# A new order of the deep layers' instruction queues, with blocks of value matmuls in pairs

## The reference

```
for i in range(6):
    x = attn_layer(shift_tokens(x), Wqkv[i], q_scale[i], k_scale[i], Wo[i]) + x
    x = ffn_layer(shift_tokens(x), ln_g[i], ln_b[i], W1[i], b1[i], W2[i], b2[i]) + x
# attn_layer: q, k, v = split(x @ Wqkv), 16 heads of 64
#             q, k = rotary(l2norm(q) * qs), rotary(l2norm(k) * ksc)
#             sim = 8 * q @ k.T   in windows of 32 with the window before
#             softmax(mask(sim)) @ v, then @ Wo
# ffn_layer:  xn = layernorm(x); a, gate = split(xn @ W1 + b1)
#             (a * gelu(gate)) @ W2 + b2
```

## Time and profile before

| | |
|---|---|
| median of 3 runs | 3265.14 us (3257.32 to 3265.72) |
| the profiled execution | 3262.19 us |
| its span, first to last instruction | 3260.4 us |
| PE busy | 3129.7 us, 96% |
| PEld busy | 2384.6 us, 73% |
| DVE busy | 2687.9 us, 82% |
| ACT busy | 2717.7 us, 83% |
| POOL busy | 2560.2 us, 79% |
| PE's share of the chain that ended last | 93% |
| granted TensorE clock, mean | 0.995 of full speed |

### The profile page before, as it was taken

How to read it: one execution, slowest core, us unless ns; L and a number is a source line. 1 busy time by engine, 2 the same in 40 slices (tenths; PEclk the granted TensorE clock), 3 DMA queues, 4 the chain that set the end, 5 groups by cost and what they waited for, 6 DMA issues and landing times.

```text
span 3260.4 us, 154019 instructions
## 1 busy us (share of the span) xinstructions
PE 3129.7 (96%) x65394; PEld 2384.6 (73%) x66148; DVE 2687.9 (82%) x4034; ACT 2717.7 (83%) x4817; POOL 2560.2 (79%) x2557
## 2 busy tenths in 40 slices
PE   8998799999999999999999999999999999999998
PEld 6886577777777777777777777777777777677776
DVE  6887888888888888888888888888888888788884
ACT  5665688888888888888888888888888888888886
POOL 3433988888888888888888888887888888788882
PEclk9999999999999999999999999999999999999999
DMA  1000332232233223223322322322332332332231
GB/s 47 29 2 28 83 79 73 75 78 68 71 75 86 69 71 80 70 64 88 82 61 74 79 67 77 85 70 63 78 78 72 78 75 67 86 75 62 65 76 52
DMA packets 140219, 224.69 MB, mean 69 GB/s; under 512 B 29456, under 2 KB 41360, under 8 KB 139152
## 3 DMA queue, kind: packets, MB, share of 16 engines
q1 hardware_dynamic: 139536, 214.78, 25.8%
HBM read 21.72 MB, written 4.19 MB: 8 GB/s over the span
## 4 chain that ended last, share of the span: by engine, by line
PE 93%; issue 3%; DVE 1%; POOL 1%; ACT 1%; DMA 0%; SPq 0%; POOLq 0%; DVEq 0%; ACTq 0%
PE bank L1021 12%; PE bank L954 11%; PE bank L906 11%; PE bank L1037 10%; PE bank L980 9%; PE bank L1367 8%; PE bank L907 7%; PE bank L999 5%; PE bank L1380 4%; PE bank L905 3%; PE bank L364 2%; PE bank L344 2%; PE bank L329 2%; PE bank L1352 1%; PE bank L1342 1%
## 5 line engine op out<-in xcount | busy, mean ns | idle before, releaser
L1284 POOL TENSOR_TENSOR rotbuf<-mbuf 128x512 f32<-128x512 f32 x768 | 975.1, 1275 | 340.4 <-PE bank L954 326.2
L1173 DVE TENSOR_TENSOR mbuf<-bank,table 128x512 f32<-128x512 f32 x768 | 522.5, 680 | 341.2 <-ACT sq L1063 290.0
L1298 POOL TENSOR_TENSOR rotbuf<-rotbuf,rs 128x512 f32<-128x512 f32 x768 | 788.9, 1043 | 14.9
L1063 ACT ACTIVATE sq<-bank 128x512 f32<-128x512 f32 x768 | 458.8, 597 | 154.7 <-PE bank L907 140.4
L1174 DVE TENSOR_TENSOR mbuf<-bank,table 128x512 f32<-128x512 f32 x768 | 522.8, 681 | 0.0
L906 PE MATMUL bank<-weights,inputs 128*128 128x512 bf16 x1152 | 438.4, 381 | 70.3 <-issue 45.3
L1021 PEld LDWEIGHTS bank<-probs_t,vbuf 64*64 64x64 f32 x24576 | 394.5, 134 | 115.7 <-issue 115.1
L954 PE MATMUL bank<-ident,rotbuf 128*128 128x128 f32 x3072 | 449.3, 279 | 17.6 <-POOL rotbuf L1298 7.8
L1155 DVE TENSOR_REDUCE ss<-sq 128x16 f32<-128x1024 f32 x384 | 459.4, 1196 | 0.0
L907 PE MATMUL bank<-weights,inputs 128*128 128x512 bf16 x1152 | 438.2, 380 | 0.0
L1021 PE MATMUL bank<-probs_t,vbuf 64*64 64x32 f32 x24576 | 437.3, 220 | 0.1
(11 more groups left out here) (119 smaller groups left out, 5736.5 us busy)
## 6 DMA issues: line engine op xcount, KB each, us to landing
vbuf<-v_stage SPq DMA_DIRECT2D x1152, 128.0 KB, 2.4
vbuf<-v_stage SPq DMA_DIRECT2D x576, 64.0 KB, 2.1
stage<-in_wqkv SPq DMA_DIRECT2D x36, 256.0 KB, 3.0
weights<-in_wo SPq DMA_DIRECT2D x6, 512.0 KB, 3.9
out_t<-weights SPq DMA_DIRECT2D x1, 2048.0 KB, 6.3
weights<-out_t SPq DMA_DIRECT2D x1, 2048.0 KB, 11.5
out_t<-weights SPq DMA_DIRECT2D x16, 128.0 KB, 2.0
wffn<-in_w SPq DMA_DIRECT2D x6, 341.0 KB, 3.1
```

Of the source, the lines that this page charges most:

```text
L1173: e.tensor_tensor(b.m1[:, u % 2, :].rearrange("p (h s d) -> p h s d", h=8, s=2), pj, cos, ALU.mult)
L1284: e.tensor_tensor(b.rot[:, u, :], b.m1[:, u % 2, :], b.m2[:, u % 2, :], ALU.add).then_inc(s.rotated, 1)
L1298: e.tensor_tensor(v, v, r, ALU.mult).then_inc(s.scaled, 1)
```

## The change

Every queue of the deep part except SP's gets a new order, and `WORK_RING` and POOL's reach follow it. No step is added or taken out, and no step changes inside. In the old order each small block on TensorE, of values or of scores, stands between large matmuls. In the new one the value blocks may stand in pairs, 128 matmul records together, and score blocks still stand alone: V2 and V3 follow each other, and V0 and V1. Of the diff, the lines that pair the value blocks, and POOL's reach:

```diff
 def pe_deep_slot(e, s, b, at):
...
-    pe_ff_mean(e, s, b, at, -1)
+    pe_ff_variance(e, s, b, at, -1)
     pe_values_of(e, s, b, at, 0, 2)
-    pe_project_in(e, s, b, at, 3, 1)
-    pe_ff_variance(e, s, b, at, -1)
     pe_values_of(e, s, b, at, 0, 3)
-    pe_ff_down(e, s, b, at, -2)
     pe_transpose(e, s, b, at, 2, 0)
...
+    pe_project_in(e, s, b, at, 3, 7)
     pe_values_of(e, s, b, at, 1, 0)
+    pe_values_of(e, s, b, at, 1, 1)
+    pe_transpose(e, s, b, at, 2, 7)
...
-POOL_REACH = (-1, 3)
+POOL_REACH = (-2, 3)
```

More of the change, by code:

```diff
@@ L1597, in pe_deep_slot @@
 def pe_deep_slot(e, s, b, at):
[L1599 to L1602, removed]
+    pe_values_in(e, s, b, at, 2, 1)
     pe_project_in(e, s, b, at, 3, 0)
     pe_transpose_probs_of(e, s, b, at, 0, 2)
-    pe_transpose(e, s, b, at, 1, 7)
+    pe_project_in(e, s, b, at, 3, 1)
+    pe_ff_mean(e, s, b, at, -1)
     pe_scores_of(e, s, b, at, 1, 1)
+    pe_ff_down(e, s, b, at, -2)
     pe_transpose_probs_of(e, s, b, at, 0, 3)
-    pe_values_in(e, s, b, at, 2, 1)
-    pe_ff_mean(e, s, b, at, -1)
+    pe_ff_variance(e, s, b, at, -1)
     pe_values_of(e, s, b, at, 0, 2)
-    pe_project_in(e, s, b, at, 3, 1)
-    pe_ff_variance(e, s, b, at, -1)
     pe_values_of(e, s, b, at, 0, 3)
-    pe_ff_down(e, s, b, at, -2)
     pe_transpose(e, s, b, at, 2, 0)
-    pe_transpose(e, s, b, at, 2, 1)
     pe_project_in(e, s, b, at, 3, 2)
@@ L1619, in pe_deep_slot @@
     pe_values_in(e, s, b, at, 2, 2)
+    pe_transpose(e, s, b, at, 2, 1)
+    pe_scores_of(e, s, b, at, 1, 3)
     pe_values_in(e, s, b, at, 2, 3)
-    pe_scores_of(e, s, b, at, 1, 3)
     pe_transpose(e, s, b, at, 2, 2)
     pe_transpose(e, s, b, at, 2, 3)
+    pe_values_in(e, s, b, at, 3, 0)
     pe_project_in(e, s, b, at, 3, 3)
@@ L1626, in pe_deep_slot @@
     pe_project_out(e, s, b, at, 0)
-    pe_values_in(e, s, b, at, 3, 0)
     pe_transpose(e, s, b, at, 2, 4)
+    pe_transpose_probs_of(e, s, b, at, 1, 0)
+    pe_transpose(e, s, b, at, 2, 5)
     pe_project_in(e, s, b, at, 3, 5)
-    pe_transpose(e, s, b, at, 2, 5)
-    pe_transpose_probs_of(e, s, b, at, 1, 0)
     pe_ff_up(e, s, b, at, -1, 0)
     pe_scores_of(e, s, b, at, 2, 0)
+    pe_transpose(e, s, b, at, 2, 6)
+    pe_transpose_probs_of(e, s, b, at, 1, 1)
     pe_ff_up(e, s, b, at, -1, 1)
@@ L1635, in pe_deep_slot @@
     pe_project_in(e, s, b, at, 3, 6)
-    pe_transpose_probs_of(e, s, b, at, 1, 1)
+    pe_ff_up(e, s, b, at, -1, 2)
+    pe_project_in(e, s, b, at, 3, 7)
     pe_values_of(e, s, b, at, 1, 0)
+    pe_values_of(e, s, b, at, 1, 1)
+    pe_transpose(e, s, b, at, 2, 7)
 def act_deep_slot(e, s, b, at):
[L1642 to L1651, removed]
+    act_copy_v(e, s, b, at, 2, 0)
     act_square(e, s, b, at, 2, 3)
     act_square(e, s, b, at, 2, 4)
+    act_input_of(e, s, b, at, 3)
     act_mask(e, s, b, at, 1, 0)
-    act_input_of(e, s, b, at, 3)
     act_ff_affine(e, s, b, at, -2)
     act_exp_of(e, s, b, at, 0, 1)
-    act_copy_v(e, s, b, at, 2, 0)
     act_copy_t(e, s, b, at, 1, 4)
+    act_copy_pt_of(e, s, b, at, 0, 0)
@@ L1660, in act_deep_slot @@
+    act_copy_t(e, s, b, at, 1, 5)
     act_square(e, s, b, at, 2, 5)
-    act_copy_t(e, s, b, at, 1, 5)
-    act_copy_pt_of(e, s, b, at, 0, 0)
-    act_ff_shift(e, s, b, at, -1)
[L1664 to L1668, removed]
+    act_ff_gelu(e, s, b, at, -2, 0)
+    act_copy_t(e, s, b, at, 1, 6)
+    act_ff_gelu(e, s, b, at, -2, 1)
+    act_copy_pt_of(e, s, b, at, 0, 1)
@@ L1669, in act_deep_slot @@
+    act_square(e, s, b, at, 2, 6)
+    act_ff_shift(e, s, b, at, -1)
     act_square(e, s, b, at, 2, 7)
     act_ff_gelu(e, s, b, at, -2, 2)
+    act_copy_t(e, s, b, at, 1, 7)
+    act_copy_v(e, s, b, at, 2, 1)
     act_square(e, s, b, at, 3, 0)
+    act_seed(e, s, b, at, 2)
+    act_square(e, s, b, at, 3, 1)
     act_copy_pt_of(e, s, b, at, 0, 2)
+    act_ff_square(e, s, b, at, -1)
     act_copy_out(e, s, b, at, 0, 0)
-    act_copy_t(e, s, b, at, 1, 7)
-    act_seed(e, s, b, at, 2)
     act_copy_pt_of(e, s, b, at, 0, 3)
-    act_copy_v(e, s, b, at, 2, 1)
@@ L1678, in act_deep_slot @@
-    act_ff_square(e, s, b, at, -1)
-    act_square(e, s, b, at, 3, 1)
     act_ff_seed(e, s, b, at, -1)
+    act_mask(e, s, b, at, 1, 1)
+    act_copy_t(e, s, b, at, 2, 0)
+    act_square(e, s, b, at, 3, 2)
+    act_exp_of(e, s, b, at, 1, 0)
+    act_copy_v(e, s, b, at, 2, 2)
+    act_copy_t(e, s, b, at, 2, 1)
+    act_copy_out(e, s, b, at, 0, 1)
+    act_copy_v(e, s, b, at, 2, 3)
+    act_copy_t(e, s, b, at, 2, 2)
+    act_copy_t(e, s, b, at, 2, 3)
 def dve_deep_slot(e, s, b, at):
-    dve_clamp(e, s, b, at, 2)
@@ L1686, in dve_deep_slot @@
     dve_rope(e, s, b, at, 3, 0)
+    dve_ff_centre(e, s, b, at, -1)
     dve_max_of(e, s, b, at, 1, 0)
-    dve_ff_centre(e, s, b, at, -1)
+    dve_rope(e, s, b, at, 3, 1)
     dve_shift(e, s, b, at, 1, 0)
-    dve_rope(e, s, b, at, 3, 1)
     dve_ff_refine(e, s, b, at, -1)
@@ L1694, in dve_deep_slot @@
     dve_sum_squares(e, s, b, at, 3, 0)
+    dve_rope(e, s, b, at, 3, 2)
     dve_sum_of(e, s, b, at, 1, 0)
-    dve_rope(e, s, b, at, 3, 2)
     dve_max_of(e, s, b, at, 1, 1)
@@ L1700, in dve_deep_slot @@
     dve_rope(e, s, b, at, 3, 4)
+    dve_sum_squares(e, s, b, at, 3, 1)
     dve_residual_of(e, s, b, at, 0)
-    dve_sum_squares(e, s, b, at, 3, 1)
+    dve_sum_of(e, s, b, at, 1, 1)
     dve_rope(e, s, b, at, 3, 5)
-    dve_sum_of(e, s, b, at, 1, 1)
-    dve_sum_squares(e, s, b, at, 3, 2)
     dve_ff_gate(e, s, b, at, -1, 0)
     dve_ff_gate(e, s, b, at, -1, 1)
+    dve_sum_squares(e, s, b, at, 3, 2)
     dve_rope(e, s, b, at, 3, 6)
+    dve_ff_gate(e, s, b, at, -1, 2)
     dve_rope(e, s, b, at, 3, 7)
-    dve_ff_gate(e, s, b, at, -1, 2)
     dve_sum_squares(e, s, b, at, 3, 3)
+    dve_clamp(e, s, b, at, 3)
 def pool_deep_slot(e, s, b, at):
+    pool_scale(e, s, b, at, 1, 3)
     pool_scale(e, s, b, at, 1, 4)
+    pool_rotate(e, s, b, at, 2, 1)
+    pool_normalise_of(e, s, b, at, 0, 0)
+    pool_rotate(e, s, b, at, 2, 2)
+    pool_ff_norm(e, s, b, at, -2)
     pool_scale(e, s, b, at, 1, 5)
+    pool_scale(e, s, b, at, 1, 6)
     pool_rotate(e, s, b, at, 2, 3)
+    pool_scale(e, s, b, at, 1, 7)
+    pool_rotate(e, s, b, at, 2, 4)
+    pool_normalise_of(e, s, b, at, 0, 1)
+    pool_rotate(e, s, b, at, 2, 5)
     pool_input_of(e, s, b, at, 3)
[L1720 to L1724, removed]
     pool_rotate(e, s, b, at, 2, 6)
@@ L1732, in pool_deep_slot @@
     pool_scale(e, s, b, at, 2, 2)
[L1733 to L1737, removed]
 def sp_deep_slot(e, s, b, at):
```

## The result

The changed kernel takes 3529.95 us (median of 4 runs, 3523.34 to 3539.99) where the kernel before took 3261.23 in the same runs: a ratio of 1.0828, 95% interval 1.0814 to 1.0842. I had forecast 3269, in a range of 3222 to 3304. The prediction was wrong, and by a term that is not in its sum.

The account below looks back on a forecast made before the run. TensorE, busy 96% of the span, was taken to bound the kernel. Paired value blocks -43, late instruction pages +54, today's stops -13, pages inside pairs +2, a freed bank +4 gave +4 us: forecast 3269, range 3222 to 3304.

Parts of the forecast that it names:

- Other moves: All queues: only places move, counts stay; one tight chain, the mean's bank freed by line 1470, charged +4 us.
- the same sum that I made for S3: TensorE's distance from the fourth value block's end to the fourth score block: 3.21 us in the new order, 5.33 before.
- Rival 2: Instruction pages behind the fourth value block held longer, most slots losing 2.1 us, not 1.7: 3296 us, chance 0.25.
- Rival 3: Bank of the mean freed 0.2 us late by line 1470 in every slot, +18 instead of +4: 3283 us, chance 0.08.
- The pairs: TensorE's paired value blocks save entries, ways out and longer following blocks: 0.48 us a slot, -43 us, from -25 to -50.
- Late pages: TensorE stops at the fourth score block, its instruction packet held behind SP's copies: +54 us in some 32 slots.
- +54 and -13 and +2: New stops for late instruction pages +54 us; today's stops not paid again -13; pages running out inside paired blocks +2.
- Rival 1: Instruction pages not late, as fewer fetches meet SP's group of copies or arrive ahead of it: 3226 us, chance 0.24.

Follow-up runs that it names:

- the changed order with its ring opened: Changed kernel, with ScalarE's copy of line 1095 waiting only for the five transfers that read its own half of the staging buffer, not all ten: 3230.69 us, 0.9918.

## Why the prediction was wrong, step by step

- **Other moves: the step that failed.** It said that "the counts of instructions and copies on ACT, DVE, POOL and SP stay; only places move, and SP's order stays as it is", and followed one chain, that of line 1470. That chain was harmless (0.2 us by its name at a projection). The move that cost 294 us in this order (89 in the old one) was costed at nothing, without naming its cover: v0 ahead of the output projection. What I left out could be worked out, in sign though not in size, from rows I had. SP's group begins at V3's end and issues a transfer every 0.63 us, so the tenth begins some 5.8 us after V3; that the first five had landed helped nobody, because line 1094 waits for all ten. From its issue a transfer takes 2.1 to 2.4 us to land, by the page of the kernel before (the last number; the tenth is one of 64 KB):

```profile
vbuf<-v_stage SPq DMA_DIRECT2D x1152, 128.0 KB, 2.4
vbuf<-v_stage SPq DMA_DIRECT2D x576, 64.0 KB, 2.1
```

With 0.6 for the copy the bank is free 8.5 to 8.8 us after V3. Before, it was a later transpose group that took v0's bank. Now it was the output projection, due 7.5 us after V3 by the same sum that I made for S3: 3.21, S3 and v3 1.4, two transposes 0.9, three projections 1.95. The difference, 1.0 to 1.3, is a wait in every slot, about 100 us; 2.37 a slot was measured. On average over the 90 slots the tenth transfer was issued only 7.0 us after V3, since one or two of the ten issues took over 0.9 us; the copy began 2.5 us later, and the projection was due at 7.8. What makes an issue take longer is not shown. The lower clock came on top.
- **None of the rivals was it.** Rival 2, worse late pages, was a mechanism of some tens of microseconds. Rival 3 was a bank that is freed late, but another bank and 18 us.
- **The pairs: right, and mis-sized.** -57 us instead of -43, outside the bounds of -25 to -50. The second block of a pair costs less than I took: 0.95 and 1.05 us for the two, 2.00 instead of 2.04; and the down projection behind S1 costs 1.40 us where I took 1.47. V2 and V3 stand as 128 records in 2.0 us, as said.
- **Late pages: the right kind, the wrong cause and size.** I had +54 and -13 and +2, +43 net; measured, +19. The packet that I placed at 3.2 us after V3's end starts in the new order mostly at 1.0 to 2.1, so S3 is stopped for 12 us and not for 54, and S2, which I left out, for 13. V3 itself, for which I gave 2 us, stops for 12 us, since a pair takes a page's 256 records in 2 us. One such stop in the changed kernel:

```profile
2529.71 1.95 PE L1021 MATMUL bank<-probs_t,vbuf 64*64 64x32 f32 x119
2532.57 0.36 PE L1021 MATMUL bank<-probs_t,vbuf 64*64 64x32 f32 x9 [0.91 <-issue]
2532.86 0.66 PE L954 MATMUL bank<-ident,rotbuf 128*128 128x128 f32 x4
```

- **Rival 1, by the rule of the Trainium skill** (Runtime: NRT & Kernel Launch, Instruction fetch mechanics: crossings "mostly hidden"), gave 3226, near the 3231 of the changed order with its ring opened. That is no proof of the rule: the stops are there, 44 us of them, and larger pair gains pay for part of them. Rows and rule differ, and the rows decide.

What stays open: what makes a packet start late when its page begins just ahead of large matmuls. It follows TensorE's order (mostly 3.2 to 3.4 us after V3 in the old one, 1.0 to 2.1 in the new), and, for most packets, not SP. Whether the sequencer asks late or is answered late the traces don't tell.

## What to carry to other kernels

When an order changes, go through every semaphore wait that a moved step issues or frees, on every queue, and give each its due time before and after; "only places move" is the sentence behind which the cost hides. A wait that counts a whole group of transfers where it needs half of it is slack that costs nothing until someone comes near it; making it narrower turned 8% slower into 0.8% faster. And a rest of TensorE can cost more than its length: look at the granted clock behind it.

## What the hardware showed that I had not expected

- A rest of 2.88 us ahead of the output projection was followed by three microseconds at a granted clock of 0.50; one of 1.18 us in the same place was followed by 1.00, and so was one of 2.71 us. On average the projection took 0.90 us longer in the changed kernel.
- An instruction packet started 3.3 us after V3's end with no other transfer running, and where S3 was stopped, TensorE went on 1.3 to 1.4 us after such a packet had landed. Where a page begins just ahead of a few large matmuls and small blocks follow, TensorE can run out of instructions. Moving transfers out of the way took 0.17 us off the packet (1.25 to 1.08 us) and 0.6 us off the start of a few, but left the start of most where it was.
